# Moving the constants of the norms from VectorE to GpSimd in two attention stages of a two-layer decoder

## What is computed

```python
x = x + _L0_attn_ref(_layernorm(x), ...)     # attention over channels
x = x + _L0_xattn_ref(_layernorm(x), ctx)    # 32 heads of 8, norms of q and k
x = x + _L0_ffn_ref(_layernorm(x), weight)   # linear layer, quantised
x = x + _L1_attn_ref(_layernorm(x), ...)     # linear attention, 16 heads of 16
x = x + _L1_xattn_ref(ctx, ctx, _layernorm(x), ...)  # long convolution
x = x + _L1_ffn_ref(_layernorm(x), ...)      # grouped attention, 8 experts
```

```python
x = o * jax.nn.sigmoid(gate)
ms = jnp.mean(xg * xg, axis=-1, keepdims=True)
xg = xg * jax.lax.rsqrt(ms + EPS)            # EPS 1e-6
o = xg.reshape(b, n, d) * weight; return o @ Wo
```

## Time and profile before

| | us |
|---|---|
| median of 3 runs | 1222.44 (1220.46 to 1223.41) |
| the profiled execution, its own time | 1228.56 |
| its span in the profile | 1226.7 |

### The profile page before, as it was taken

The page is one execution under the profiler, slowest core; times in us unless marked ns, Lnnn a source line. Parts: engine busy times, 40 slices in busy tenths (PEclk is TensorE's granted clock), DMA queues, the critical chain, the costliest instruction groups (busy, mean ns, idle before and its releaser), DMA issues.

```text
span 1226.7 us, 26308 instructions
## 1 busy us (share of the span) xinstructions
PE 1141.5 (93%) x8174; PEld 886.4 (72%) x8175; DVE 774.5 (63%) x1938; ACT 562.1 (46%) x1502; POOL 603.1 (49%) x751
## 2 busy tenths in 40 slices
PE   7998999978999789988999999999997999999996
PEld 5776666644555434477887888888886879999995
DVE  4555688867888679975776676777666643222221
ACT  3444777852333200035666666666665652222221
POOL 2102566635655457754566666666564523323323
PEclk9999999989999889999999999999998999999999
DMA  7000000006999040030000000000001138888884
GB/s 286 1 0 9 15 15 15 11 2 133 186 195 179 1 178 1 4 137 2 6 14 14 14 14 17 13 13 21 13 14 52 53 110 230 243 238 240 239 233 97
DMA packets 57272, 99.88 MB, mean 81 GB/s; under 512 B 5809, under 2 KB 44017, under 8 KB 56433
## 3 DMA queue, kind: packets, MB, share of 16 engines
q1 hardware_dynamic: 42432, 62.92, 20.6%
q10 hardware_dynamic: 7616, 26.74, 6.0%
q0 software_dynamic: 7152, 9.34, 4.3%
HBM read 87.53 MB, written 30.48 MB: 96 GB/s over the span
## 4 chain that ended last, share of the span: by engine, by line
PE 51%; DMA 14%; issue 12%; DVE 8%; ACT 5%; POOLq 4%; POOL 4%; DVEq 2%; ACTq 0%
DMA out<-g.spare,ex.token 13%; PE bank L2231 9%; PE bank L2119 8%; PE bank L2144 4%; PE bank L2128 3%; PE bank L512 2%; PE bank L2195 2%; PE bank L1184 2%; PE bank L1355 2%; PE bank L1356 2%; PE bank L2137 2%; PE bank L1357 2%; PE bank L1251 1%; PE bank L1242 1%; ACT ga.e L1987 1%
## 5 line engine op out<-in xcount | busy, mean ns | idle before, releaser
L2119 PEld LDWEIGHTS bank<-ga.xnT,g.early 128*128 128x128 f32 x1280 | 153.1, 195 | 7.7 <-issue 7.7
L2119 PE MATMUL bank<-ga.xnT,g.early 128*128 128x128 f32 x1280 | 158.4, 278 | 0.0
L1744 POOL TENSOR_TENSOR ga.halves<-ga.halves,g.ga_sinT 128x512 f32<-128x512 f32 x80 | 103.4, 1292 | 62.3 <-ACT ga.halves L1980 62.3
L2231 PE MATMUL bank<-g.early,ga.aT 128*128 128x256 f32 x512 | 117.0, 382 | 0.5 <-ACT ga.aT L2002 0.5
L1987 ACT ACTIVATE ga.e<-bank,ga.negmax 128x128 f32<-128x128 f32 x256 | 90.4, 366 | 50.9 <-DVE ga.negmax L1841 49.9
L1752 POOL TENSOR_TENSOR ga.kqT<-ga.by_cos,ga.halves 128x512 f32<-128x512 f32 x80 | 102.4, 1280 | 16.0 <-issue 16.0
L2231 PEld LDWEIGHTS bank<-g.early,ga.aT 128*128 128x128 f32 x512 | 94.9, 190 | 12.3 <-ACT ga.aT L2002 0.7
L1828 DVE TENSOR_TENSOR ga.by_cos<-bank,g.ga_cosT 128x512 f32<-128x512 f32 x80 | 55.2, 691 | 68.1 <-PE bank L2119 49.4
L2360 DVE TENSOR_TENSOR g.spare<-g.spare,bank 128x512 f32<-128x512 f32 x39 | 26.8, 688 | 97.6 <-PE bank L2417 93.2
L2144 PE MATMUL bank<-ga.pT,ga.v 128*128 128x512 f32 x128 | 69.2, 623 | 14.1 <-ACT ga.pT L1995 13.8
L2408 PEld LDWEIGHTS bank<-g.spare 128*128 128x128 f32 x624 | 75.6, 192 | 1.9
(11 more groups left out here) (311 smaller groups left out, 2621.5 us busy)
## 6 DMA issues: line engine op xcount, KB each, us to landing
g.spare<-in_mo_w SPq DMA_DIRECT2D x39, 512.0 KB, 4.3
g.spare<-in_mo_w ACTq DMA_DIRECT2D x39, 512.0 KB, 4.7
mo_rows<-in_pad_rows SPq DMA_DIRECT2D x1, 18447.0 KB, 109.0
g.spare<-mo_rows SPq DMA_DIRECT2D x39, 129.0 KB, 3.2
g.late<-in_mo_w SPq DMA_DIRECT2D x1, 4096.0 KB, 13.6
g.ctxT<-in_ctxR SPq DMA_DIRECT2D x1, 2048.0 KB, 13.7
xa.ctxT<-in_ctxT SPq DMA_DIRECT2D x16, 128.0 KB, 2.6
g.spare<-cv_rows SPq DMA_DIRECT2D x1, 2048.0 KB, 8.0
```

The source lines that it names most:

```text
L1744: nc.gpsimd.tensor_tensor(by_sin[:, par, :].rearrange("p (h t) -> p h t", h=REP), halves[:, par, :].rearrange("p (h t) -> p h t", h=REP), ...
L2119: last = nc.tensor.matmul(pkq[:, par, j * P:(j + 1) * P], w[:, q, at * P:(at + 1) * P], xnT[:, s.par, q, :], start=(q == 0), stop=(q == C ...
L2231: last = nc.tensor.matmul(pout, aT[:, h // REP, (h % REP) * P:(h % REP + 1) * P], g.ga_wo[:, h, :], start=(h == 0), stop=(h == H - 1))
```

## The change

In both attention stages VectorE no longer adds the constant of a layer norm: `layer_norm_moments` ends with the aggregation, and `layer_norm_root` on GpSimd adds the constant from a small tile g.eps, drains, and takes the root. The group norm's squares are only summed on VectorE; GpSimd adds 16 x 4e-6 and takes the root, and the missing factor of 16 under the root is made good by multiplying the output weights by 4. Channel attention keeps the old form. In `xa`, the root of the next layer norm moves on GpSimd from ahead of the norms of q and k to the end of the step. In `la`, VectorE's addition to x moves from the end of a step to behind la.u of the next one; the product with the decay is issued in two halves; TensorE multiplies the first half with the values ahead of the transposes of la.un and the second behind them.

```diff
@@ -215,6 +215,7 @@
     g.minus_half = m.sb("minus_half", [P, 1])
+    g.eps = m.sb("eps", [P, 2])
     early = m.sb("early", [P, 12288])
@@ -314,15 +315,30 @@
         def _(pool):
+            nc.gpsimd.memset(g.eps[:, 0:1], LN_EPS)
+            nc.gpsimd.memset(g.eps[:, 1:2], 16 * 4e-6)
             nc.gpsimd.memset(g.minus_half[:], -0.5).then_inc(g.fill, 1)
...
 
-def layer_norm_stats(nc, m, x_b, par, eps_var_ready):
+def layer_norm_moments(nc, m, x_b, par):
 
...
     dve.drain()
-    nc.vector.bn_aggr(m.mv[:, par, 0:2], m.stats[:, par, :])
+    return nc.vector.bn_aggr(m.mv[:, par, 0:2], m.stats[:, par, :])
+
+
+def layer_norm_root(nc, pool, g, m, par):
+
+    nc.gpsimd.tensor_tensor(m.mv[:, par, 2:3], m.mv[:, par, 1:2], g.eps[:, 0:1], ALU.add)
+    pool.drain()
+    return nc.gpsimd.tensor_tensor(m.rstd[:, par, :], m.mv[:, par, 2:3], g.minus_half[:], ALU.pow)
+
+
+def layer_norm_stats(nc, m, x_b, par, eps_var_ready):
+
+    dve = nc.vector
+    layer_norm_moments(nc, m, x_b, par)
     dve.drain()
@@ -631,14 +647,7 @@
                 pool.wait_ge(q_var_ready, upto(c))
-                nc.gpsimd.tensor_tensor(n.rstd[:, c.par, :], n.mv[:, c.par, 2:3], g.minus_half[:],
-                                        ALU.pow).then_inc(q_rstd_ready, 1)
-            if n2.on:
-                pool.wait_ge(var_ready, upto(n2))
-                if n2.past(2):
-                    pool.wait_ge(xn_ready, upto(n2, back=2))
-                nc.gpsimd.tensor_tensor(m.rstd[:, n2.par, :], m.mv[:, n2.par, 2:3], g.minus_half[:],
-                                        ALU.pow).then_inc(rstd_ready, 1)
+                layer_norm_root(nc, pool, g, n, c.par).then_inc(q_rstd_ready, 1)
             if s.on:
@@ -650,6 +659,11 @@
                 nc.gpsimd.tensor_tensor(g.x[:, a.i, :], g.x[:, a.i, :], o[:, a.par, :], ALU.add).then_inc(x_added, 1)
+            if n2.on:
+                pool.wait_ge(var_ready, upto(n2))
+                if n2.past(2):
+                    pool.wait_ge(xn_ready, upto(n2, back=2))
+                layer_norm_root(nc, pool, g, m, n2.par).then_inc(rstd_ready, 1)
         return Part(step, 2, 4, before)
@@ -674,7 +688,7 @@
                 for k in range(C):
-                    last = nc.vector.tensor_scalar(g.la_wo[:, k, :], g.la_wo[:, k, :], g.la_norm[:, k:k + 1], None, ALU.mult)
+                    last = nc.vector.tensor_scalar(g.la_wo[:, k, :], g.la_wo[:, k, :], g.la_norm[:, k:k + 1], 4.0, ALU.mult, ALU.mult)
                 last.then_inc(g.la_wo_ready, 1)
@@ -688,12 +702,12 @@
                     dve.wait_ge(xn_ready, upto(n2, back=2))
-                layer_norm_stats(nc, m, g.x[:, n2.i, :], n2.par, var_ready)
+                layer_norm_moments(nc, m, g.x[:, n2.i, :], n2.par).then_inc(var_ready, 1)
             if s.base is None and s.n == 1:
...
                 dve.wait_ge(x_added, upto(c))
-                layer_norm_stats(nc, n, g.x[:, c.i, :], c.par, q_var_ready)
+                layer_norm_moments(nc, n, g.x[:, c.i, :], c.par).then_inc(q_var_ready, 1)
             if b.on:
@@ -957,7 +971,7 @@
     u, usq = m.sb("u", [P, D]), m.sb("usq", [P, D])
-    msq, norm = m.sb("msq", [P, H]), m.sb("norm", [P, H])
+    msq, mean_sq, norm = m.sb("msq", [P, H]), m.sb("mean_sq", [P, H]), m.sb("norm", [P, H])
     un, unT = m.sb("un", [P, D]), m.sb("unT", [P, C, P])
@@ -1010,11 +1024,12 @@
                 pool.wait_ge(var2_ready, upto(c))
-                nc.gpsimd.tensor_tensor(n2.rstd[:, c.par, :], n2.mv[:, c.par, 2:3], g.minus_half[:],
-                                        ALU.pow).then_inc(rstd2_ready, 1)
+                layer_norm_root(nc, pool, g, n2, c.par).then_inc(rstd2_ready, 1)
             if a.on:
                 pool.wait_ge(msq_ready, upto(a))
-                nc.gpsimd.tensor_tensor(norm[:], msq[:], g.minus_half[:].broadcast_to([P, H]), ALU.pow).then_inc(norm_ready, 1)
+                nc.gpsimd.tensor_tensor(mean_sq[:], msq[:], g.eps[:, 1:2].broadcast_to([P, H]), ALU.add)
+                pool.drain()
+                nc.gpsimd.tensor_tensor(norm[:], mean_sq[:], g.minus_half[:].broadcast_to([P, H]), ALU.pow).then_inc(norm_ready, 1)
             if s.on:
@@ -1025,8 +1040,7 @@
                     pool.wait_ge(xn_ready, upto(b, back=2))
-                nc.gpsimd.tensor_tensor(m.rstd[:, b.par, :], m.mv[:, b.par, 2:3], g.minus_half[:],
-                                        ALU.pow).then_inc(rstd_ready, 1)
+                layer_norm_root(nc, pool, g, m, b.par).then_inc(rstd_ready, 1)
         return Part(step, 2, 3, before)
@@ -1041,6 +1055,9 @@
                                                op0=ALU.add, op1=ALU.mult).then_inc(u_ready, 1)
+            if c.on:
+                dve.wait_ge(out_done, upto(c))
+                nc.vector.tensor_tensor(g.x[:, c.i, :], pout, g.x[:, c.i, :], ALU.add).then_inc(x_added, 1)
             if b.on:
@@ -1049,14 +1066,12 @@
                 dve.drain()
-                layer_norm_stats(nc, n2, g.x[:, c.i, :], c.par, var2_ready)
+                layer_norm_moments(nc, n2, g.x[:, c.i, :], c.par).then_inc(var2_ready, 1)
             if a.on:
...
                     dve.wait_ge(norm_ready, upto(a, back=1))
-                nc.vector.tensor_reduce(msq[:], usq[:].rearrange("p (h d) -> p h d", d=HD), AX.X, ALU.add)
-                dve.drain()
-                nc.vector.tensor_scalar(msq[:], msq[:], 1.0 / HD, 4e-6, ALU.mult, ALU.add).then_inc(msq_ready, 1)
+                nc.vector.tensor_reduce(msq[:], usq[:].rearrange("p (h d) -> p h d", d=HD), AX.X, ALU.add).then_inc(msq_ready, 1)
             n = s.back(-1)
@@ -1076,8 +1091,10 @@
                     dve.wait_ge(xa.pv_done, B)
-                nc.vector.tensor_tensor(a_mat[b.par], ps[:].rearrange("p r n -> p (r n)"),
-                                        g.la_decay.rearrange("p h t -> p (h t)"), ALU.mult).then_inc(a_ready, 1)
+                for k in range(C):
+                    nc.vector.tensor_tensor(a_mat[b.par].rearrange("p (r k n) -> p r k n", r=4, k=C)[:, :, k, :], ps[:, :, k * D:(k + 1) * D],
+                                            g.la_decay.rearrange("p (r k h) t -> p r k (h t)", r=4, k=C)[:, :, k, :],
+                                            ALU.mult).then_inc(a_ready, 1)
             if a.on:
@@ -1097,10 +1114,7 @@
                     dve.wait_ge(xn_ready, upto(n, back=2))
-                layer_norm_stats(nc, m, g.x[:, n.i, :], n.par, var_ready)
-            if a.on:
-                dve.wait_ge(out_done, upto(a))
-                nc.vector.tensor_tensor(g.x[:, a.i, :], pout, g.x[:, a.i, :], ALU.add).then_inc(x_added, 1)
+                layer_norm_moments(nc, m, g.x[:, n.i, :], n.par).then_inc(var_ready, 1)
         return Part(step, 2, 3)
@@ -1161,6 +1175,16 @@
 
+        def masked_values(b, k):
+            pe.wait_ge(a_ready, upto_part(b, C, k))
+            for q in range(2):
+                for r in range(4):
+                    at, head = q * 256 + (k * 4 + r) * 32, (r * 2 + k) * 2 + q
+                    last = nc.tensor.matmul(po[32 * r:32 * r + 32, k, :],
+                                            vd[:, b.par, :, :].rearrange("p q y -> p (q y)")[:, at:at + 32],
+                                            a_mat[b.par][:, head * P:(head + 1) * P], start=(q == 0), stop=(q == 1))
+            return last
+
         def step(s):
@@ -1189,7 +1213,7 @@
                 if b.past(1):
-                    pe.wait_ge(a_ready, upto(b, back=1))
+                    pe.wait_ge(a_ready, upto(b, back=1, per=C))
                 else:
@@ -1223,6 +1247,9 @@
                 s.meet()
+            if b.on:
+                pe.wait_ge(v_ready, upto(b))
+                masked_values(b, 0)
             if a.on:
@@ -1233,16 +1260,7 @@
             if b.on:
-                pe.wait_ge(v_ready, upto(b))
-                pe.wait_ge(a_ready, upto(b))
-                for k in range(C):
-                    for q in range(2):
-                        for r in range(4):
-                            at, head = q * 256 + (k * 4 + r) * 32, (r * 2 + k) * 2 + q
-                            last = nc.tensor.matmul(po[32 * r:32 * r + 32, k, :],
-                                                    vd[:, b.par, :, :].rearrange("p q y -> p (q y)")[:, at:at + 32],
-                                                    a_mat[b.par][:, head * P:(head + 1) * P], start=(q == 0), stop=(q == 1))
-                last.then_inc(av_done, 1)
+                masked_values(b, 1).then_inc(av_done, 1)
             if a.on:
@@ -1347,7 +1365,7 @@
                 pe.wait_ge(g.filt_loaded, 16)
-                pe.wait_ge(la.a_ready, B)
+                pe.wait_ge(la.a_ready, C * B)
             pe.wait_ge(g.kv_ready, u + 1)
```

## The result

The change took 1226.77 us in the median of 19 runs, the kernel before 1224.46 in the median of its 19 beside it: a ratio of 1.0025, with an interval from 1.0016 to 1.0034, so **3.1 us slower** (2.0 to 4.2); the plain difference of the two medians is 2.3. One run of the change, at 1243.99 us, was a slow one and stands outside the ratio. The 3.1 is inside the 0.3% that the prediction calls no change, and close to its +3.3; the 1225.7 that it named for the median was missed by 1.1, since it started from the 1222.44 of before's first three runs.

A forecast was written before the change was run, and what follows sets the result against it. No engine is full; circles of waits set the pace, VectorE with GpSimd in cross attention. Terms -2.3 + 2.0 + 1.3 + 1.7 - 0.7 + 0.6 + 0.7 = +3.3 us on 1222.44: 1225.7, range 1217.5 to 1231.

The forecast's parts named there:

- Cross attention: Looped cross attention: two VectorE constant adds gone, the VectorE and GpSimd circle no longer decides; -2.3 us over 8 steps.
- Rival D: Cross attention: gains nothing because ScalarE's qT is held by something beside VectorE; +5.6 us, 1228.0; chance 0.10.
- A small add: On GpSimd: costs its start-to-start spacing, 0.34 us for 128x1 and 0.37 for the group norm's, not its span.
- rival E: GpSimd adds cost only their span, or TensorE keeps its clock in last step; -0.7 to +1.3 us; chance 0.18.
- The loop: Linear-attention loop: GpSimd circle grows by 0.48 us, from 9.19 to 9.67; +0.25 a step for 8 steps, +2.0.
- Product steps: Two linear-attention steps with a convolution product on GpSimd: 10.07 us from qkr to qkr against 9.22; +1.7 us.
- Halves: Linear attention: halved mask product's saving hidden by the longer GpSimd circle, counting only in the last full step; -0.7 us.
- The moved addition: Linear attention: addition to x behind u costs nothing in the loop; at the very end +0.6 us with the last root.
- The junction: Between the stages: two GpSimd adds lie on the path to the last quantised block's xq; +0.7 us.
- B: Linear attention: VectorE's cn.xn and the norm's GpSimd add collide on ports; 4.5 us more, 1230.2; chance 0.12.
- C: Linear attention: GpSimd's adds are hidden and the halves pay; -8.2 us, 1214.2; chance 0.15.
- A: The forecast itself, whole kernel: all terms together +3.3 us, 1225.7; chance 0.45.

The follow-up runs named there:

- experiment one: Only the cross-attention part of the change, linear attention as in the kernel before; 1222.96 us, ratio 0.9982 to before.
- Experiment two: Only the linear-attention part of the change, cross attention as in the kernel before; 1228.52 us, ratio 1.0026 to before.
- experiment four: The change with the group norm's add on GpSimd issued twice, each behind its own drain; 1231.89 us, ratio 1.005 to before.
- experiment three: The change with the constants of linear attention's three norms back on VectorE; 1217.19 us, ratio 0.9939 to before; second run 1218.87 us, 0.9929.
- seven: Experiment three with the mask product whole and all masked values behind un's transposes; 1221.98 us, ratio 0.9995 to before.
- experiment ten: Experiment three with the addition to x back at the end of the step; 1217.43 us, ratio 0.9935 to before.
- five: The change with only the group norm's constant back on VectorE; 1219.46 us, ratio 0.996 to before.
- six: The change with only the two layer norms' constants of linear attention back on VectorE; 1222.89 us, ratio 0.9989 to before.

## Why the prediction was right

The total, +3.3 for +3.1, is right, and so is the mechanism: which circle decides, and what an add in line costs. That the two numbers agree to 0.2 us is partly luck, as the rows below show. Forecast, and measured between the same instructions of VectorE, against before and against experiment one:

| stretch | forecast | vs before | vs one |
|---|---|---|---|
| cross-attention loop | -2.3 | -2.45 | 0.0 |
| last xa.qkn to first la.qT | +0.7 | -0.7 | +0.5 |
| first to second la.qT | 0 | +1.5 | +1.1 |
| to the 6th (two product steps) | +2.1 | +1.5 | +1.6 |
| linear-attention loop | +2.0 | +1.3 | +1.2 |
| two straight-line steps | +0.9 | +1.1 | +1.1 |
| last qT to the convolution | -0.1 | -0.7 | 0.0 |

The forecast's parts in linear attention come to 5.6, the last column to 5.5, the runs to 5.3 (± 1.7). Against before the table adds up to only 1.55, since that execution took long at the junction in code that experiment one has too: 26.18 us from the last xa.qkn to the first la.qT, for 24.99.

The 5.5 is not all the change's doing, though. Experiment two has the same linear attention, and its rows come to 3.2 us against before: 0.3 from the last la.qkr of the junction to the first la.qT (it has one of the two adds there), 1.5 to the 6th la.qT, 1.3 in the loop, 0.5 in the two straight-line steps, -0.4 behind them. The change's execution repeats them but for two things. From the first to the third la.qT it took 20.29 us, 1.5 more than the 18.82 of experiment two, at the lower clock (point 7). And its two straight-line steps, 9.89 and 9.70 us for experiment two's 9.52 and 9.41, have two pauses in which the engine waited for nothing that the profile shows:

```profile
400.48 0.18 DVE L328 BATCH_NORM_AGGREGATE cn.mv<-cn.stats 128x2 f32<-128x6 f32 x1 [0.44 <-issue]
...
410.88 0.55 POOL L335 TENSOR_TENSOR cn.rstd<-cn.mv,g.minus_half 128x1 f32<-128x1 f32 x1 [0.43 <-issue]
```

Without the two, and with both adds at the junction, the rows give 0.67 + 1.53 + 1.27 + 0.46 + 0 = 3.93 for the forecast's 5.6, and with cross attention's -2.45 they explain about +1.5 of the +3.1 (2.0 to 4.2). The forecast's terms for linear attention were thus about 1.7 too high, and something that it left out made up for it. The longer spell at the lower clock and the pauses would fill the gap in this one execution; whether they come more often in the change than before, no run tells.

1. *Cross attention*, -2.3: shown by the rows of ScalarE and by experiment one. Rival D (cross attention gives nothing) is out.

2. *A small add*, 0.34 and 0.37: 0.33 and 0.35, and experiment four prices the second at 0.37 a step in the loop. Had the span been the price, as in rival E, the fourth would have cost 0.21 a step.

3. *The loop*, +2.0: +1.2 to +1.3, **the term that was mis-sized**. The circle is 9.68 in the step shown; in the other of the pair the next qT follows qkr after 370.10 - 368.09 = 2.01 us instead of 2.18, and it is 9.52. The forecast took 9.67 for the mean of the two, which is 9.58 over the loop; 0.09 in 8 steps is 0.7 us. That the circle had a slack before was right: from 9.22 and 9.16 it grew by 0.46 and 0.36, not by 0.48, and cost 0.16 a step. In the straight-line steps behind the loop, forecast at 9.65, it is 9.52 and 9.41 in experiment two, for 9.24 and 9.23 before.

4. *Product steps*, 10.07: they took 9.86 and 9.84 from qkr to qkr. The order of work is as forecast, with no gap from product to norm; only the two roots were priced at their longer form (0.62, and 3.03 with 0.04 to un; now 0.52, and 298.93 - 295.98 = 2.95 with it).

5. *Halves*: "hidden by the longer GpSimd circle" fits the loop, where un starts 0.56 us behind the mask product; three and seven show what the halves are worth with the adds away. The change without the halves was not run. From the last qT to the last un, -0.7 was forecast for the halves; the change is 0.6 under before and 0.1 under experiment one. TensorE waits 1.38 us for un there and runs the masked values and the output product at 1.2 GHz, as it did before.

6. *The moved addition*, 0 in the loop: experiment ten, where the adds are away, has 0.7 in eight steps in the move's favour. The +0.6 for the end did not come: from the last un to the last cn.xn 4.75 us, before 4.83, in experiment one 4.65. Against experiment one this miss and that of point 5 cancel.

7. *The junction*, +0.7: the wait for xq grew by 2.57 - 1.90 = 0.67, as forecast. The other traces confirm it add by add: the wait is 1.90 us with none of the two adds on the path, 2.23 or 2.24 in the nine traces with one, and 2.57 in the three with both; and from the last la.qkr ahead of it to the first la.qT it is 5.16, 5.49 or 5.50, and 5.83 us. Behind the wait TensorE is at 1.2 GHz, before as after (granted clock 0.50 over 281 to 282 there); the next four matmuls took 3.15 us before, 3.78 in the change, 2.64 in experiment one. That the longer wait caused the 3.78 would be the obvious reading. Experiment four speaks against it. Its TensorE waits the same 2.57 us:

```profile
274.31 0.28 PE L898 MATMUL bank<-g.ident_bf,ql.xq 128*128 128x128 bf16 x2 [2.57 <-POOL ql.xq L658]
...
278.05 2.79 PE L1232 MATMUL bank<-g.early,la.xnT 128*128 128x512 f32 x4
```

and takes a microsecond less for the four, with the granted clock at 1.00 again from 280, 5.7 us behind the end of the wait; in the change it is still 0.50 up to 281, 8.1 us behind it. From the first to the third la.qT ten of the thirteen traces, with none, one or both adds, take 18.75 to 18.96 us; the change takes 20.29, five 19.72 and six, with one add, 19.79. So the +1.1 of the table's third row goes with how long TensorE stayed at the lower clock in this execution, and the length of the wait does not set it. The Trainium skill ("TensorE: Matmul & The Clock Gate", HAM oscillation — how this bites in real kernels) describes how matmuls behind a long wait, there for a DMA, start at the lower clock. Here the wait is for GpSimd and the rows show the same, and they add that how long it lasts differs between executions with the same wait.

Of the rivals, B (ports) did not occur: the norm's add started at 353.40 and cn.xn at 353.46, and took 0.21 and 0.41, cn.xn as long as before. So it is in all fifteen steps that have both: the add started 0.06 to 0.08 us first, and neither was held up. C (adds hidden) was wrong in its condition, since the two adds cost what A said. Its size, 8.2 us under before without the adds, is close to the 7.5 of experiment three, but not for its reasons: it had 3.7 of it in the loop, and the trace of three has 2.3 there.

## What to carry to other kernels

Where a step is set by a circle of waits, an operation costs its start-to-start spacing if it lies in line on the circle and nothing if it runs beside it, whichever engine is the less busy: with the layer norms' constants on VectorE, moving the group norm's from the busier VectorE, where it was free, to GpSimd cost 0.37 us a step. Take a mixed change apart before keeping or dropping it, since here the halves were worth 1.7 us in the loop and 3 to 7 in all once the adds were off the circle; with the adds on it un waited for the norm, and the loop could not show it. Sum the stages against more than one trace: a total that agrees to 0.2 us can hold two errors that cancel. Then ask what the circle orders needlessly: putting the norm ahead of cn gave the fastest kernel, once its own new wait was seen and shortened; nearly all that it gained over three lies in the last step, not in the loop.

## What was not expected of the hardware

- GpSimd's 128x1 root of cn, behind its add and drain, took 0.65 or 0.66 us in every looped step and 0.55 in the two with a product (0.58 before, without an add, in the loop). Why, no run here tells.
- An add of 128x1 behind the 1.89 us product took 0.27, and the next operation started 0.41 after it instead of 0.33.
- The clock after a wait is not set by the wait alone. With TensorE idle for 2.57 us at the same place, the next four matmuls took 3.78 us in one kernel and 2.79 in another; identical code ran its last linear-attention step at either of TensorE's two clock levels in two executions, 1.85 us apart (13.55 and 15.40): in such a stretch one profile doesn't give the price of an edit.
